# Two graph layers on one core: the softmax row of the first layer goes to columns by two transfers instead of a TensorE transpose

## The reference

```
q, k = split(x @ Wqk);  v = x @ Wv
agg  = adj @ (k * mask)
w    = mask * sum(q * agg, axis=-1) / 16            # one number for each node
x1   = layernorm(x + softmax(w over the nodes)[:, None] * v)

query, key, value = x1 @ Wq.T + bq, x1 @ Wk.T + bk, x1 @ Wv.T + bv
e    = adj * exp(query @ key.T)
out  = layernorm(x1 + (e / sum(e, axis=2)) @ value)
```

## Time and profile before

| | |
|---|---|
| median of 3 runs | 296.41 us (296.34 to 297.03) |
| profiled execution | 296.95 us, its span 295.2 us |
| TensorE busy | 287.0 us, 97% of the span |
| VectorE busy | 235.1 us, 80% |
| ScalarE busy | 224.7 us, 76% |
| GpSimd busy | 220.3 us, 75% |
| one x1 sum of one graph (L630) | 480 ns |
| one x1 norm of one graph (L452) | 595 ns |
| moved by DMA | 31.26 MB, mean 106 GB/s |

### The profile page before, as it was taken

How to read it: one execution, slowest core, us unless ns; L and a number is a source line. 1 busy time by engine, 2 the same in 40 slices (tenths; PEclk the granted TensorE clock), 3 DMA queues, 4 the chain that set the end, 5 groups by cost and what they waited for, 6 DMA issues and landing times.

```text
span 295.2 us, 7074 instructions
## 1 busy us (share of the span) xinstructions
PE 287.0 (97%) x2012; PEld 266.6 (90%) x2012; DVE 235.1 (80%) x728; ACT 224.7 (76%) x539; POOL 220.3 (75%) x269
## 2 busy tenths in 40 slices
PE   7999999999999999999999999999999999999991
PEld 7789999999999999999999999999999999999980
DVE  1478888888878888888888888788887888888784
ACT  3455768788788878878887887878788787887763
POOL 1556988877888877788887778978777897877331
PEclk9999999999999999999999999999999999999997
DMA  6921234322344432324443232444323243210102
GB/s 231 338 91 37 89 92 126 93 95 85 109 124 125 125 96 86 95 96 125 125 125 92 86 101 94 125 125 125 93 85 92 103 125 125 89 55 25 50 36 107
DMA packets 19165, 31.26 MB, mean 106 GB/s; under 512 B 2128, under 2 KB 6608, under 8 KB 19152
## 3 DMA queue, kind: packets, MB, share of 16 engines
q1 hardware_dynamic: 19152, 31.11, 34.2%
HBM read 22.71 MB, written 8.39 MB: 105 GB/s over the span
## 4 chain that ended last, share of the span: by engine, by line
PE 94%; DMA 2%; issue 1%; DVE 1%; ACT 0%; POOL 0%; SPq 0%; POOLq 0%; DVEq 0%
PE ps L866 25%; PE ps L868 24%; PE ps L867 24%; PE ps L967 9%; PE ps L949 5%; DMA p<-params 2%; PE ps L917 1%; PE ps L923 1%; PE ps L889 1%; PE ps L1101 1%; PE ps L972 1%; DVE x L649 0%; PE ps L928 0%; PE ps L936 0%; POOLq L36 0%
## 5 line engine op out<-in xcount | busy, mean ns | idle before, releaser
L866 PE MATMUL ps<-w_hi,xt_hi 128*128 128x512 f32 x124 | 49.9, 402 | 0.0
L868 PE MATMUL ps<-w_hi,xt_lo 128*128 128x512 f32 x124 | 48.8, 393 | 0.0
L867 PE MATMUL ps<-w_lo,xt_hi 128*128 128x512 f32 x124 | 48.5, 391 | 0.0
L452 ACT ACTIVATE x<-x_sum,shift,rstd 128x256 f32<-128x256 f32 x60 | 32.9, 595 | 17.0 <-POOL shift L377 17.0
L363 POOL TENSOR_TENSOR edge_lo<-edge,edge_hi 128x256 fp32r<-128x256 f32 x29 | 21.5, 740 | 29.5 <-ACT edge_hi L532 29.5
L296 POOL TENSOR_TENSOR x1b<-x,bv_all 128x512 f32<-128x512 f32 x31 | 40.2, 1297 | 2.6 <-DVE x L805 1.7
L350 POOL TENSOR_TENSOR xt_lo<-xt_raw,xt_hi 128x512 fp32r<-128x512 f32 x31 | 40.1, 1294 | 1.8 <-ACT xt_hi L434 1.8
L467 ACT ACTIVATE z<-ps,z_bias 128x256 f32<-128x256 f32 x62 | 26.0, 472 | 19.7 <-PE ps L868 19.7
L374 POOL TENSOR_TENSOR rstd<-var_eps,minus_half 128x4 f32<-128x4 f32 x31 | 33.2, 1071 | 9.3 <-DVE var_eps L783 9.3
L866 PE MATMUL ps<-wv_hi,x1t_hi 128*128 128x258 f32 x124 | 37.8, 305 | 0.0
L357 POOL TENSOR_TENSOR x_lo<-x_raw,x_hi 128x512 fp32r<-128x512 f32 x28 | 36.2, 1293 | 0.0
(11 more groups left out here) (162 smaller groups left out, 880.3 us busy)
## 6 DMA issues: line engine op xcount, KB each, us to landing
xt_raw<-xt_pairs SPq DMA_DIRECT2D x32, 256.0 KB, 2.7
x_raw<-x_pairs SPq DMA_DIRECT2D x32, 256.0 KB, 2.7
out_pairs<-x SPq DMA_DIRECT2D x31, 256.0 KB, 2.0
adjt<-adjt_pairs SPq DMA_DIRECT2D x32, 129.0 KB, 2.1
p<-params SPq DMA_DIRECT2D x1, 770.0 KB, 6.7
p<-params SPq DMA_DIRECT2D x1, 512.0 KB, 3.8
p<-params SPq DMA_DIRECT2D x1, 256.0 KB, 4.7
out_pairs<-x SPq DMA_DIRECT2D x2, 128.0 KB, 1.8
```

The source lines that it names most:

```text
L452: last = nc.scalar.activation(out[:, graph(g)], in_[:, graph(g)], ACT.Identity, bias=shift[r % 2][:, layer, g:g + 1], scale=rstd[r % 2][:, ...
L866: nc.tensor.matmul(out, s_hi, m_hi, start=first, stop=False)
L867: nc.tensor.matmul(out, s_hi, m_lo, start=False, stop=False)
L868: return nc.tensor.matmul(out, s_lo, m_hi, start=False, stop=last)
```

## The change

Four things change. For pairs 3 to 30 (`by_tensor` is false) p_row is no longer transposed by TensorE; SP issues two transfers from SBUF to SBUF, one for each graph, of 128 values of 4 bytes from one partition's row of p_row to one column of p_col in 128 partitions. SP waits for p_row and then issues them between the x load and the adjacency load of its slot; each sum of x1 waits for its own transfer, and the next p_row is written only when both have landed. The transpose of the weights moves from behind the twelve query matmuls to between the first six and the last six. The row maximum moves between the two x2 operations of VectorE, the row exponential ahead of the query copies on ScalarE, and the reciprocal and p_row ahead of the statistics of x2. From slot 1 on, ScalarE writes the high part of x1 transposed from PSUM, ahead of the plain copy, and VectorE no longer casts it but subtracts from PSUM.

```diff
+def by_tensor(pair):
+    return pair < 3 or pair == PAIRS - 1
...
@@ SP, slot, behind the x load
+                if exists(t + 1) and not by_tensor(r + 1):
+                    sp.wait_ge(p_row_done, t + 2)
+                    sp.wait_ge(x1_sum_done[1], t + 1)
+                    for g in range(2):
+                        sp.dma_start(p_col[:, g:g + 1], p_row[g:g + 1, :]).then_inc(p_moved[g], 16)
@@ ScalarE, slot
                     act.wait_ge(x1t_done, t + 1)
+                    if r != 0:
+                        act.wait_ge(val_done, t)
+                        nc.scalar.copy(x1t_hi[:, :, :, :], x1t_ps).then_inc(x1t_hi_done, 1)
                     nc.scalar.copy(x1t[:, :, :, :], x1t_ps).then_inc(x1t_copied, 1)
...
+                if exists(t + 2):
+                    act.wait_ge(row_max_done, t + 3)
+                    nc.scalar.activation(exp_row_ps(r + 2), w_row_ps(r + 2), ACT.Exp, bias=neg_max[:, 0:1],
+                                         accum_out=exp_sum[:, 0:1]).then_inc(row_exp_done, 1)
                 if exists(t) and r != 0:
                     act.wait_ge(z_done, t + 1)
                     bias_z(z)
-                if exists(t + 2):
-                    act.wait_ge(row_max_done, t + 3)
-                    nc.scalar.activation(exp_row_ps(r + 2), w_row_ps(r + 2), ACT.Exp, ...)
@@ VectorE
-            def split_x1t(t):
+            def split_x1t(t, r):
                 dve.wait_ge(x1t_copied, t + 1)
-                if exists(t - 1):
-                    dve.wait_ge(val_done, t)
-                nc.vector.tensor_copy(x1t_hi[:, :, :, :], x1t[:, :, :, :]).then_inc(x1t_hi_done, 1)
+                if r == 0:
+                    nc.vector.tensor_copy(x1t_hi[:, :, :, :], x1t[:, :, :, :]).then_inc(x1t_hi_done, 1)
                 dve.wait_ge(x1t_hi_done, t + 1)
-                nc.vector.tensor_tensor(x1t_lo[:, :, :, :], x1t[:, :, :, :], ...
+                nc.vector.tensor_tensor(x1t_lo[:, :, :, :], x1t[:, :, :, :] if r == 0 else x1t_ps, ...
             def sum_x1(u, r):
+                if by_tensor(r): ... (the wait and the copy from PSUM as before)
                 for g in range(2):
+                    if not by_tensor(r):
+                        dve.wait_ge(p_moved[g], 16 * u - 32)
                     nc.vector.scalar_tensor_tensor(out=x1_sum[r % 2][:, graph(g)], ...
@@ VectorE, slot
                     for g in range(2):
+                        if g == 1 and exists(t + 2):
+                            row_max(t + 2, r + 2)
                         last = nc.vector.scalar_tensor_tensor(out=x2[(r - 1) % 4][:, graph(g)], ...
...
+                if exists(t + 2):
+                    dve.wait_ge(row_exp_done, t + 3)
+                    nc.vector.reciprocal(inv_sum[:, :], exp_sum[:, :]).then_inc(inv_sum_done, 1)
+                    dve.wait_ge(inv_sum_done, t + 3)
+                    if by_tensor(r + 1):
+                        dve.wait_ge(p_col_done, t + 2)
+                    elif exists(r + 1):
+                        for g in range(2):
+                            dve.wait_ge(p_moved[g], 16 * t - 16)
+                    nc.vector.tensor_scalar(p_row[0:2, :], exp_row_ps(r + 2), inv_sum[:, 0:1], None, ALU.mult)\
+                        .then_inc(p_row_done, 1)
                 if exists(t - 1):
                     dve.wait_ge(x2_done, t)
                     both_stats(1, x2[(r - 1) % 4]).then_inc(stats2_done, 1)
-                (reciprocal and p_row stood here)
@@ TensorE
-            def queries(hi, lo):
+            def queries(hi, lo, weighted=None):
                 for m in range(HALVES):
+                    if m == 1 and weighted:
+                        transpose_w(*weighted)
...
-                    queries(x1t_hi, x1t_lo)
-                if exists(t + 2) and r > 0:
-                    transpose_w(t + 2, r + 2)
+                    queries(x1t_hi, x1t_lo, (t + 2, r + 2) if exists(t + 2) and r > 0 else None)
...
                 if r != DRAIN:
-                    transpose_p(t + 2, r + 2)
+                    if by_tensor(r + 2):
+                        transpose_p(t + 2, r + 2)
                     transpose_next(t, r)
```

More of the change, by code:

```diff
@@ L142, in build @@
         ident_zeroed, ident_ready, consts_ready = sem("ident_zeroed"), sem("ident_ready"), sem("consts_ready")
-        p_row_zeroed = sem("p_row_zeroed")
+        p_row_zeroed, p_moved = sem("p_row_zeroed"), sems("p_moved", 2)
         bqk_done, bqk_summed, ones_ready = sem("bqk_done"), sem("bqk_summed"), sem("ones_ready")
@@ L562, in slot @@
                          first_half_normed if r == -1 else None)
-                if exists(t) and r != 0:
-                    act.wait_ge(z_done, t + 1)
-                    bias_z(z)
                 if exists(t + 2):
@@ L570, in slot @@
                                          accum_out=exp_sum[:, 0:1]).then_inc(row_exp_done, 1)
+                if exists(t) and r != 0:
+                    act.wait_ge(z_done, t + 1)
+                    bias_z(z)
                 if exists(t + 3) and r + 3 >= SPLIT:
@@ L612, in both_stats @@
                                           source[:, :].rearrange("p (g d) -> p d g", g=2))
-            def split_x1t(t):
+            def split_x1t(t, r):
                 dve.wait_ge(x1t_copied, t + 1)
-                if exists(t - 1):
-                    dve.wait_ge(val_done, t)
-                nc.vector.tensor_copy(x1t_hi[:, :, :, :], x1t[:, :, :, :]).then_inc(x1t_hi_done, 1)
+                if r == 0:
+                    nc.vector.tensor_copy(x1t_hi[:, :, :, :], x1t[:, :, :, :]).then_inc(x1t_hi_done, 1)
                 dve.wait_ge(x1t_hi_done, t + 1)
-                nc.vector.tensor_tensor(x1t_lo[:, :, :, :], x1t[:, :, :, :], x1t_hi[:, :, :, :].bitcast(F32),
+                nc.vector.tensor_tensor(x1t_lo[:, :, :, :], x1t[:, :, :, :] if r == 0 else x1t_ps, x1t_hi[:, :, :, :].bitcast(F32),
                                         ALU.subtract).then_inc(x1t_lo_done, 1)
             def sum_x1(u, r):
-                dve.wait_ge(p_col_done, u + 1)
-                nc.vector.tensor_copy(p_col[:, :], p_col_ps(r)).then_inc(p_copied, 1)
+                if by_tensor(r):
+                    dve.wait_ge(p_col_done, min(u + 1, 4))
+                    nc.vector.tensor_copy(p_col[:, 0:2], p_col_ps(r)).then_inc(p_copied, 1)
                 if exists(u - 2):
                     dve.wait_ge(x1_done, u - 1)
-                dve.wait_ge(p_copied, u + 1)
+                if by_tensor(r):
+                    dve.wait_ge(p_copied, min(u + 1, 4))
                 for g in range(2):
+                    if not by_tensor(r):
+                        dve.wait_ge(p_moved[g], 16 * u - 32)
                     nc.vector.scalar_tensor_tensor(
@@ L749, in drain, with row_max @@
                                             ALU.add, ALU.mult).then_inc(last_out_done, 1)
+            def row_max(u, r):
+                dve.wait_ge(w_row_done, u + 1)
+                nc.vector.tensor_reduce(neg_max[:, :], w_row_ps(r), AX.X, ALU.max, negate=True).then_inc(row_max_done, 1)
             def slot(t, r):
                 if r == 0:
-                    split_x1t(t)
+                    split_x1t(t, r)
                 if exists(t + 1):
@@ L812, in slot @@
                     nc.vector.tensor_copy(s_bias[:, :], bias_ps[:, HALVES:HALVES + 1]).then_inc(biases_ready, 1)
-                if exists(t + 2):
-                    dve.wait_ge(w_row_done, t + 3)
-                    nc.vector.tensor_reduce(neg_max[:, :], w_row_ps(r + 2), AX.X, ALU.max, negate=True).then_inc(row_max_done, 1)
+                if exists(t + 2) and not exists(t - 1):
+                    row_max(t + 2, r + 2)
                 if r == 0:
                     normed_x1(1, 0, norms(0))
-                if exists(t - 1):
-                    dve.wait_ge(x2_done, t)
-                    both_stats(1, x2[(r - 1) % 4]).then_inc(stats2_done, 1)
                 if exists(t + 2):
@@ L826, in slot @@
                     dve.wait_ge(inv_sum_done, t + 3)
-                    if exists(t + 1):
+                    if by_tensor(r + 1):
                         dve.wait_ge(p_col_done, t + 2)
+                    elif exists(r + 1):
+                        for g in range(2):
+                            dve.wait_ge(p_moved[g], 16 * t - 16)
                     nc.vector.tensor_scalar(p_row[0:2, :], exp_row_ps(r + 2), inv_sum[:, 0:1], None, ALU.mult)\
                         .then_inc(p_row_done, 1)
+                if exists(t - 1):
+                    dve.wait_ge(x2_done, t)
+                    both_stats(1, x2[(r - 1) % 4]).then_inc(stats2_done, 1)
                 if exists(t) and r != DRAIN:
```

## The result

| | before | changed |
|---|---|---|
| median of the runs | 296.72 us (5 runs) | 298.92 us (298.17 to 299.31, 5 runs) |
| ratio | | 1.0072, 95% interval 1.0053 to 1.0091 |
| profiled execution, its span | 296.95, 295.2 | 298.92, 297.1 |
| mean slot, t = 7 to 26 | 8.629 | 8.665 |
| the slots of t = 4 and 5 together | 17.20 | 18.60 |

The time lies 0.1 us above the upper end of the range; the forecast was 293.3, and the mechanism that came true is rival 1's: the first sum of x1 starts late, behind its transfer, and TensorE waits for it.

A forecast was written before the change was run, and what follows sets the result against it. TensorE was taken as the bound, busy for all 43.00 us of steady state. Removing 28 transposes of 0.11 us saves 3.1: span 295.2 to 292.1, plus 1.75 around it 293.85, median 0.54 lower: 293.3 us, range 292.3 to 298.8.

The forecast's parts named there:

- rival 1: Landing takes 2.0 to 2.1 us, TensorE waits for the first sum every slot: 298.6 us at 2.0, 301.4 at 2.1; chance 0.22.
- The landing: First SBUF-to-SBUF transfer, from issue to arrival: 1.6 us taken from stores, bounds 1.5 and 2.1, arriving at P + 7.65.
- 6.68 + landing: Slot length through the transfer; a slot lasts max(8.49, 6.68 + landing), with no loss up to a landing of 1.81 us.
- The rest of the path: After landing, VectorE wakes (0.05) and sums (0.48) to P + 8.18; TensorE needs it 0.08 ahead, 0.02 to wake: P + 8.28.
- The issue at P + 6.05: SP issues the first transfer 6.05 us after slot start P: row written at P + 5.83, wake 0.18, second wait 0.05.
- The Trainium skill's fixed cost: About 2.0 us for any transfer, stated for GpSimd's path; by it a slot is 8.68 and the kernel 2.2 us slower.
- step of 0.11: Probability row's transpose leaves TensorE's queue, saving 0.11 us in 28 of 32 pairs: 3.1 us, slot 8.49.
- Base of the slot: Time from one pair's first projection product to the next pair's before the change: 8.60 us, TensorE busy throughout.
- slack of 0.1 us: Before the change, the first x1 sum ends about 148.27, some 0.1 us before the next slot's first product loads weights at 148.40.
- ScalarE's copy at nothing: High part of x1 transposed moves to ScalarE, adding 0.5 us there, covered by its 1.5 us idle a slot: no cost.
- Second transfer: Issued about 0.54 after the first, lands at P + 8.2; its sum ends 0.2 into the next slot, as before.
- Query copies and x2: ScalarE's query copies at P + 5.3 to 6.15 and VectorE's x2 by P + 5.28, before the scores at P + 6.45: no cost.

The follow-up runs named there:

- row-to-row run: Changed kernel with each transfer writing its 128 values to one row instead of a column, and the sums of x1 reading a ready column of ones: 294.01 us, one run.
- ready column: Changed kernel with the sums of x1 for pairs 3 to 30 reading a column of ones already in SBUF, transfers still issued: 293.78 us, ratio 0.989.
- experiment 7: Changed kernel with the hardware loop starting at slot 8 instead of slot 4, to study the long slots 4 and 5: 298.86 us, ratio 1.0074.

## Why the prediction was wrong, step by step

- **The landing was the step that failed**: 1.6 us taken, 1.93 measured for the first transfer (mean of t = 7 to 26). By the prediction's own formula, 6.68 + landing, that is a slot of 8.61 instead of 8.49, as long as before: this step alone takes back the whole gain of 3.1 us. Its bounds of 1.5 and 2.1 held it, and it fell just past the break-even of 1.92; the chance of 0.22 for rival 1 was too small for a term that was never measured. The 1.6 came from large stores. A transfer of 512 B to a row does land in 1.63, so what the extrapolation missed is the shape: the column's 112 small packets more, 0.3 us.
- **The rest of the path**: the measured slot is 8.665, not 8.61. The first transfer is issued at 6.08 instead of 6.05, the sum starts 0.02 behind the landing, and from the sum's start to the product it takes 0.63, where 0.58 was taken (0.48 for the sum, 0.10 for TensorE).
- **The issue at P + 6.05** was nearly hit (6.08) by two errors that cancel: SP wakes in 0.03, not 0.23, and the row ends at 6.05, not 5.83. The 0.05 for a second wait on SP is in no run. The difference in the row is mostly the two waits ahead of it (0.16), which I had read in the diff and counted at nothing; the run without them is 3.4 us faster.
- **The Trainium skill's fixed cost** of about 2.0 us (DMA: Bandwidth & Descriptors, Anatomy of one DMA), there for another path, is close to what this trace shows for SP's transfers to a column: 1.93 and 2.04. The row-to-row run, 1.63 and 1.72 for as many bytes, shows that it isn't the same for every shape.
- **The sign that misled.** The prediction said that TensorE's list would show 28 waits for the sums if the landing was wrong, and that slots of 8.6 with no wait would mean that the step of 0.11 was wrong. The list shows one wait and slots of 8.665, and the landing was wrong all the same: a stall this short (the slot is 0.16 us longer than with the ready column) makes no entry. The weight load's lead (0.03 instead of 0.08) and the constant 0.63 from sum to product show it.
- **Base of the slot.** I took 8.60 from one slot. The mean before is 8.629: before too, at the loop's branch, the sum starts late (8.02 to 8.06 into the slot) and the slot lasts 8.65 to 8.69, 0.63 behind it. The slack of 0.1 us was already used up once in four slots.
- **Transpose of 0.11 us**: right; 8.506 with the ready column, 8.49 computed. In one sum ScalarE's busy time in five slots stands as 35.2 us and is 35.29; nothing hangs on it.
- **ScalarE's copy at nothing**: wrong both ways, -2.3 us with the transfers, +1.1 without.
- **Second transfer**: it was to land at P + 8.2 and its sum to end 0.2 into the next slot. It is issued at 6.62 and lands at 8.66, and the sum ends 0.50 into the next slot. The x1 norm behind it, which was to keep its place (4.49), ends at 4.73 to 4.79. In the steady slots the row maximum ends at 4.83, so this cost next to nothing there; in slot 5 it cost the 0.7 us of experiment 7. Query copies and x2: right, no run shows a wait of TensorE for them.
- **The sum after the fact**: 28 slots (t = 1 to 28) took 243.8 us against 241.5. The two long slots are 1.4 of it, the 26 others 0.8, or 0.03 each. So rival 1's price (298.6 at a landing of 2.0) is near the 298.9 by luck: the steady part was cheaper than it said, and the late landings it didn't contain.

## What to carry to other kernels

Moving 0.1 us of work off the bound engine onto a transfer buys it only if the whole detour, issue to landing to the consumer, fits in the slack that the work had; measure the landing of that very shape first, because 512 B to one column took 1.9 to 2.0 us here, about as long as a store of 256 KB. Find the first consumer that the bound engine waits for (here: the sum that frees a bank) and follow it in one slot, since "97% busy" is the same with and without the stall. On such a path waits count even if they are always satisfied: two of them, with a count computed from the loop's register behind the reciprocal, took 0.16 us of VectorE's time in each slot and decided between 0.7% slower and 0.5% faster.

## What was not expected of the hardware

- The two transfers of 512 B: issue 0.48 us for the first and 0.60 for the second on SP (0.33 for 256 KB), landing 1.9 to 2.1 in the steady state, 144 packets to a column and 32 to a row.
- Two waits that are already satisfied cost 0.16 us on VectorE in a looped slot, where an instruction for the count (40 to 53 ns) comes with them, and nothing in the unrolled slots (rows at 5.86 against 6.05).
- Landings of 2.4 to 3.6 us for both transfers of a pair came only when a load of 16 KB of instructions started 0.4 to 1.3 us behind the first one's issue; whether it is the cause wasn't settled.
